# Normalised rows transposed by the DMA crossbar as fp16 halves, in place of TensorE in fp32

## The chip, the cores and the metric

The kernel runs on one core of a Trainium2 chip. A core has five engines that run programs of their own: TensorE (matrix products; PE in the profile, its weight loads PEld), VectorE (DVE), ScalarE (ACT), GpSimd (POOL) and SyncE (SP), which here does nothing but issue DMAs. They wait for each other on semaphores. The metric is the device time of one execution in microseconds (us); before the change it is 2462.75 us, the median of three runs (2460.89 to 2462.85).

## The reference

Input are 128 graphs of 128 nodes with 256 features (`x`) and their adjacency matrices. After a LayerNorm and a ReLU three layers follow, and the input is added at the end:

```
for l in range(3):
    scores = leaky(x@attn_w[l,:d] [:, :, None] + x@attn_w[l,d:] [:, None, :] + attn_b[l])
    attn = softmax(where(mask, scores, -inf))
    h = layernorm(x + attn @ x, g1[l], beta1[l])
    x = layernorm(h + gelu(h @ W1[l] + b1[l]) @ W2[l] + b2[l], g2[l], beta2[l])
```

Everything is float32. W1 is 256 x 1024 and W2 1024 x 256.

## The kernel before

Four graphs (T = 4) make a group; a group in one layer is an item, with 512 rows. There are 32 groups and 96 items. They are taken in rings of four groups: four items of layer 0, four of layer 1, four of layer 2, so twelve slots (PER) make one ring. Products are done in fp16 with both operands split into a high and a low half (hi = fp16(v), lo = v - hi), as three products hi*hi, hi*lo and lo*hi.

A software pipeline over slots sets the order. In slot s every engine goes through eight chunks c = 0..7. At each chunk TensorE does `hidden(s, c)`: 128 of the 1024 hidden features for the 512 rows, six matmuls (L369) with the transposed normalised rows `hT_hi`, `hT_lo` as moving operand; the first four use `hT_hi`, the last two `hT_lo`, and at c = 0 each pair is preceded by a wait for its half. ScalarE makes the GELU (L481) and the high half (L486), VectorE the low half (L573), and TensorE does `feed` of the chunk three earlier (12 matmuls, L383). Between the chunks stands the work of other items:

- item s+2: dot products for the scores on VectorE (L614, L617, c = 1), their spread over the rows by TensorE (L407, c = 4), scores, row maxima and `minus_max` on VectorE (L632 to L642, c = 4), leaky scores and exponentials on ScalarE (L509, L514, c = 5), the transpose of the probabilities on TensorE (L413, c = 7), their split (L519, L666), and in the next slot at c = 0, after `feed`, the aggregation (L425). VectorE then makes `res1` (L656) and its statistics (L580).
- item s+1: inverse deviation on GpSimd (L789, L791), `norm1` on ScalarE (L491, c = 2), its transpose on TensorE (`transpose_norm1`, L435, c = 4), `hT_hi` on ScalarE (L535, c = 4), `hT_lo` on VectorE (L671, c = 5), and on GpSimd the residual (L801, L803). The transpose is eight 128 x 128 transposes in fp32 into four PSUM banks of `p_pair`, which are shared with `feed` and the aggregation, so it waits for `res2` of item s-1.
- item s-1: residual `res2` (L681), statistics, normalisation and output on VectorE and GpSimd (L815, L827, L829, and L836 after the last layer).
- item s+4, where a new group starts (layer 0, `starts` in VectorE's program, four slots of twelve): statistics of the input and mask on VectorE (L580, L601, L604).

PSUM is full: three banks for `hidden`, one for the scores and probabilities, four for `p_pair`.

SyncE's program is written group by group: it waits until `x_in` and `adj_in` of a group are used up and loads the group two further on, then waits for an output, stores it, and loads `x` again for the sum at the end. Within the loop its addresses come from a register.

The lines of the prediction's steps are those named above; the waits of the low half at TensorE are L367 and L368, and the six matmuls of a chunk are issued in the loop at L365.

Of the kernel before, what the change touches and what calls it, by code (L numbers as in the profile page):

```python
# [35 lines left out]
P = 128  # L36
B, N, D = 128, 128, 256
L = 3
# [21 lines left out]
def layer_of(s):  # L60
    return (s % PER) // RING
# [35 lines left out]


def is_item(r, s):
    return not isinstance(r, int) or 0 <= PER * r + s < ITEMS  # L100
# [29 lines left out]
def gnn_kernel(nc, x, adj, attn_w, attn_b, W1, b1, W2, b2, g1, beta1, g2, beta2, out):  # L130
    with ExitStack() as ctx:
# [55 lines left out]
        h_res = [sb(f"h_res{i}", [P, T, D]) for i in range(2)]  # L187
        hT_hi = [sb(f"hT_hi{i}", [P, KD, TN], F16) for i in range(2)]
        hT_lo = [sb(f"hT_lo{i}", [P, KD, TN], F16) for i in range(2)]
        g_hi = [sb(f"g_hi{i}", [P, TN], F16) for i in range(GS_RING)]  # L190
# [20 lines left out]
        def ff_banks(s):  # L211
            return p_pair[s % 2]

        def nT_banks(s):
            return p_pair[s % 2][:].rearrange("p (k u) d -> p k (u d)", k=KD)

# [31 lines left out]
        norm1_ready = sem("norm1_ready")  # L248
        nT_psum = sem("nT_psum")
        hT_hi_ready = sem("hT_hi_ready")  # L250
# [23 lines left out]
        @block.sync  # L274
        def _(sp):
            def weights(l):
                if l >= 1:
                    sp.wait_ge(w_lo_ready, 4 * l - 2)
                    sp.wait_ge(bias_psum, l)
                sp.dma_start(w1_f32[:], W1[l].rearrange("(k p) h -> p k h", p=P)).then_inc(w_dma[0], 16)  # L280
                if l >= 1:
                    sp.wait_ge(w_lo_ready, 4 * l)
                sp.dma_start(w2_f32[:], W2[l].rearrange("(c p) d -> p c d", p=P)).then_inc(w_dma[1], 16)

            def graphs(tensor, g):

                v = tensor.rearrange("(g t) n d -> n g t d", t=T)
                if isinstance(g, int):
                    return v[:, g]
                return v[:, bass.ds(g, 1)].rearrange("n g t d -> n (g t) d")  # L290

            def load_x(g, i):
                sp.dma_start(x_in[i][:], graphs(x, g)).then_inc(x_loaded[i], 16)

            def load_adj(g, i):
                sp.dma_start(adj_in[i][:], graphs(adj, g)).then_inc(adj_loaded[i], 16)

            def load_again(g, i):
                sp.dma_start(x_again[i][:], graphs(x, g)).then_inc(x_again_loaded[i], 16)

            def store(g, i):
                sp.dma_start(graphs(out, g), y_out[i][:]).then_inc(stored[i], 16)

            load_x(0, 0)
            load_adj(0, 0)
# [7 lines left out]
            load_x(1, 1)  # L313
            load_adj(1, 1)
            weights(0)
            for g in (2, 3, 4, 5):
                sp.wait_ge(x0_ready, 4 * (g - 1))
                load_x(g, g % 2)
                sp.wait_ge(mask_steps, 2 * (g - 1))
                load_adj(g, g % 2)  # L320
                if g == 2:
                    for dst, v in ((g1_rows, g1), (b2_rows, b2), (res_rows, beta1), (g2_rows, g2), (beta2_rows, beta2)):
                        sp.dma_start(dst[:].rearrange("p l d -> p (l d)"),
                                     flat(v).partition_broadcast(P)).then_inc(rows_dma, 16)
                if g in (3, 4):
                    weights(g - RING + 2)
            load_again(0, 0)
            load_again(1, 1)

            for r in range(LOOPS - 1):  # L330
                for q in range(RING):
                    i, g = q % 2, r * RING + q

                    sp.wait_ge(x0_ready, r * (4 * RING) + 4 * (RING + q + 1))
                    load_x(g + (RING + 2), i)
                    sp.wait_ge(mask_steps, r * (2 * RING) + 2 * (RING + q + 1))
                    load_adj(g + (RING + 2), i)

                    sp.wait_ge(x_steps, x_total(r, 2 * RING + q, 5))
                    store(g, i)  # L340
                    load_again(g + 2, i)
            for g in range(RING * (LOOPS - 1), G):
                if g + RING + 2 < G:
                    sp.wait_ge(x0_ready, 4 * (g + RING + 1))
                    load_x(g + RING + 2, g % 2)
                    sp.wait_ge(mask_steps, 2 * (g + RING + 1))
                    load_adj(g + RING + 2, g % 2)
                sp.wait_ge(x_steps, x_total(g // RING, 2 * RING + g % RING, 5))
                store(g, g % 2)
                if g + 2 < G:  # L350
                    load_again(g + 2, g % 2)
            for i in range(2):
                sp.wait_ge(stored[i], 16 * G // 2)

        @block.tensor
        def _(pe):
            def hidden(r, s, c):

                l, i = layer_of(s), s % 2
                if c == 0:  # L360
                    pe.wait_ge(hT_hi_ready, total(r, s, 1, 1))
                if later(r, s) or c >= PF_RING:
                    pe.wait_ge(g_lo_ready, total(r, s, C, c + 1 - PF_RING))
                cols = slice(c * P, (c + 1) * P)
                for n, (w, h, k) in enumerate((w, h, k) for w, h in ((w1_hi, hT_hi), (w1_lo, hT_hi), (w1_hi, hT_lo))  # L365
                                              for k in range(KD)):
                    if c == 0 and n == 2 * KD:  # L367
                        pe.wait_ge(hT_lo_ready, total(r, s, 1, 1))  # L368
                    mm = pe.matmul(p_hid[in_ring(s, c, PF_RING)][:], w[l][:, k, cols], h[i][:, k, :],  # L369
                                   start=(n == 0), stop=(n == 3 * KD - 1))  # L370
# [45 lines left out]
            def aggregate(r, s):  # L416

                pe.wait_ge(pT_lo_ready, total(r, s, 1, 1))
                pe.wait_ge(X_lo_ready, total(r, s, 1, 1))
                if later(r, s):  # L420
                    pe.wait_ge(hT_lo_ready, total(r, s - 1, 1, 1))
                for t in range(T):
# [16 lines left out]
            def slot(r, s):  # L439
                for c in range(C):  # L440
# [13 lines left out]
                    if c == 4 and first:  # L454
                        spread_sj(r, s + 2)
                    if c == 4 and is_item(r, s + 1):
                        transpose_norm1(r, s + 1)
                    if c == 4 and is_item(r, s + 2) and not first:
# [8 lines left out]
        def _(act):  # L467
# [61 lines left out]

            def high_hT(r, s):  # L530

                act.wait_ge(nT_psum, total(r, s, 1, 1))
                if later(r, s, 2):
                    act.wait_ge(hid_psum, total(r, s - 2, C, C))
                act.activation(hT_hi[s % 2][:], nT_banks(s), ACT.Copy).then_inc(hT_hi_ready, 1)  # L535

            def slot(r, s):
                if isinstance(r, int) and r == 0 and s in (0, 3):
                    act.wait_ge(bias_ready, 1 if s == 0 else L)
                for c in range(C):  # L540
# [8 lines left out]
                    if c == 4 and is_item(r, s + 1):  # L549
                        high_hT(r, s + 1)  # L550
                    if c == 5 and is_item(r, s + 2):
# [9 lines left out]
        def _(dve):  # L561
# [106 lines left out]

            def split_hT(r, s):
                dve.wait_ge(hT_hi_ready, total(r, s, 1, 1))  # L670
                dve.tensor_tensor(hT_lo[s % 2][:], nT_banks(s), hT_hi[s % 2][:], ALU.subtract).then_inc(hT_lo_ready, 1)  # L671

# [33 lines left out]
            def slot(r, s):  # L706
# [7 lines left out]
                for c in range(C):  # L714
# [33 lines left out]
                    if c == 5 and is_item(r, s + 1):  # L748
                        split_hT(r, s + 1)
                    if c == 5 and starts and not late:  # L750
# [128 lines left out]
```

## Time and profile before

| | us |
|---|---|
| median of 3 runs | 2462.75 |
| the profiled execution | 2464.22 |
| its span | 2462.4 |
| TensorE busy | 2350.7 (95%) |
| VectorE busy | 2097.8 (85%) |
| ScalarE busy | 1890.0 (77%) |
| GpSimd busy | 1701.0 (69%) |

The granted TensorE clock is 0.993 of full speed over the span. An engine's busy time doesn't say whether it sets the time; that is read from the chain of waits, which follows the last instruction back through what released it. The rows are below.

### The profile page before, as it was taken

The page shows a single profiled execution, that of the slowest core. Times are in us where ns is not written, and L with a number is a line of the kernel's source. Part 1 is how long each engine was busy: PE and PEld are TensorE (multiplying, and loading weights), DVE is VectorE, ACT ScalarE, POOL GpSimd, SP SyncE. Part 2 cuts the span into 40 slices and gives each one's busy share as a digit, 9 for nine tenths or more (in the row PEclk, how much of TensorE's full clock was granted, in tenths as well). Part 3 has the DMA queues.
Part 4 walks back from the last instruction along what each step waited for, and adds up shares of the span by engine and source line. Part 5 has one row for each costly group of instructions (what it writes and reads, how often), then busy time and mean ns, then how long its engine had stood idle before and what let it go on. Part 6 is the DMA issues. An engine that isn't in the chain of part 4 may idle for free.

```text
span 2462.4 us, 47718 instructions
## 1 busy us (share of the span) xinstructions
PE 2350.7 (95%) x16608; PEld 1648.4 (67%) x16608; DVE 2097.8 (85%) x6070; ACT 1890.0 (77%) x3402; POOL 1701.0 (69%) x1540
## 2 busy tenths in 40 slices
PE   3999999999999999999999999999999999999997
PEld 2766666676666666667666666666666666666765
DVE  6778998888988899888988889988898889988884
ACT  4767788877787878787787777877778777878783
POOL 3457677767776767766786667776678676777675
PEclk9999999999999999999999999999999999999998
DMA  5200012000210002100021001200012000110001
GB/s 170 73 1 1 1 44 78 1 1 1 74 48 1 1 14 61 48 1 1 14 78 31 1 1 31 73 18 2 1 44 61 18 2 1 44 52 1 1 1 52
DMA packets 77422, 70.84 MB, mean 29 GB/s; under 512 B 7040, under 2 KB 75648, under 8 KB 77184
## 3 DMA queue, kind: packets, MB, share of 16 engines
q1 hardware_dynamic: 77184, 67.79, 9.1%
q8 instruction: 134, 2.20, 0.4%
q14 instruction: 104, 0.85, 0.1%
HBM read 51.01 MB, written 16.78 MB: 28 GB/s over the span
## 4 chain that ended last, share of the span: by engine, by line
DVE 55%; PE 19%; ACT 13%; issue 10%; POOL 0%; DVEq 0%; POOLq 0%
DVE g_lo L573 11%; DVE bn L580 9%; PE p_pair L383 8%; DVE res L656 6%; DVE dots L614 6%; ACT probs L514 5%; PE p_hid L369 5%; ACT L514 5%; DVE res L681 5%; DVE scores L632 4%; DVE dots L617 4%; PE p_pair L425 3%; DVE row_top L638 3%; DVE minus_max L642 2%; PE p_att L413 2%
## 5 line engine op out<-in xcount | busy, mean ns | idle before, releaser
L383 PE MATMUL p_pair<-w_hi,g_hi 128*128 128x256 f16 x3072 | 839.1, 273 | 0.0
L383 PE MATMUL p_pair<-w_lo,g_hi 128*128 128x256 f16 x3072 | 838.8, 273 | 0.0
L383 PE MATMUL p_pair<-w_hi,g_lo 128*128 128x256 f16 x3072 | 838.8, 273 | 0.0
L481 ACT ACTIVATE p_hid<-p_hid,b_eff 128x512 f32<-128x512 f32 x768 | 504.5, 657 | 328.6 <-PE p_hid L369 327.4
L573 DVE TENSOR_TENSOR g_lo<-p_hid,g_hi 128x512 f16<-128x512 f32 x768 | 527.5, 687 | 239.4 <-ACT g_hi L486 232.9
L801 POOL TENSOR_TENSOR h_res<-norm,g_rows 128x1024 f32<-128x1024 f32 x96 | 227.7, 2372 | 395.8 <-DVE res L681 389.1
L486 ACT ACTIVATE g_hi<-p_hid 128x512 f16<-128x512 f32 x768 | 458.5, 597 | 24.3
L369 PE MATMUL p_hid<-hT_hi,w_hi 128*128 128x512 f16 x1536 | 458.7, 380 | 2.3 <-DVE g_lo L573 2.3
L369 PE MATMUL p_hid<-hT_hi,w_lo 128*128 128x512 f16 x1536 | 458.9, 380 | 0.0
L369 PE MATMUL p_hid<-hT_lo,w_hi 128*128 128x512 f16 x1536 | 458.8, 380 | 0.0
L789 POOL TENSOR_TENSOR rstd<-var_eps,minus_half 128x4 f32<-128x4 f32 x224 | 241.6, 1079 | 307.4 <-DVE minus_mean L588 302.1
L383 PEld LDWEIGHTS p_pair<-w_lo,g_hi 128*128 128x128 f16 x3072 | 301.2, 98 | 107.3 <-issue 0.8
L383 PEld LDWEIGHTS p_pair<-w_hi,g_hi 128*128 128x128 f16 x3072 | 301.2, 98 | 106.2 <-issue 1.0
L383 PEld LDWEIGHTS p_pair<-w_hi,g_lo 128*128 128x128 f16 x3072 | 301.2, 98 | 35.5
L491 ACT ACTIVATE norm<-res,shift,rstd 128x256 f32<-128x256 f32 x384 | 199.3, 589 | 102.0 <-POOL shift L791 102.0
L369 PEld LDWEIGHTS p_hid<-hT_lo,w_hi 128*128 128x128 f16 x1536 | 150.8, 98 | 182.6 <-issue 2.5
L369 PEld LDWEIGHTS p_hid<-hT_hi,w_lo 128*128 128x128 f16 x1536 | 150.7, 98 | 182.5 <-issue 2.2
L580 DVE BATCH_NORM_STATS2 bn<-res 128x6 f32<-128x256 f32 x768 | 268.9, 414 | 3.3
L803 POOL TENSOR_TENSOR h_res<-h_res,res_rows 128x1024 f32<-128x1024 f32 x96 | 226.9, 2363 | 7.5
L587 DVE TENSOR_SCALAR var_eps<-mv 128x4 f32<-128x4 f32 x224 | 213.4, 953 | 7.7
L815 POOL TENSOR_SCALAR norm<-res,rstd,shift 128x256 f32<-128x256 f32 x384 | 209.8, 561 | 10.0
L656 DVE SCALAR_TENSOR_TENSOR res<-p_pair,row_inv,X 128x256 f32<-128x256 f32 x384 | 159.0, 477 | 65.5 <-PE p_pair L425 65.5
(67 smaller groups left out, 3855.2 us busy)
## 6 DMA issues: line engine op xcount, KB each, us to landing
x_in<-in_x SPq DMA_DIRECT2D x32, 512.0 KB, 5.3
x_again<-in_x SPq DMA_DIRECT2D x32, 512.0 KB, 5.1
out<-y_out SPq DMA_DIRECT2D x32, 512.0 KB, 3.3
adj_in<-in_adj SPq DMA_DIRECT2D x32, 256.0 KB, 5.6
w_f<-in_L_gnn_W SPq DMA_DIRECT2D x6, 1024.0 KB, 5.6
attn_rows<-in_L_gnn_attn_w SPq DMA_DIRECT2D x1, 768.0 KB, 5.6
g_rows<-in_L_gnn_g SPq DMA_DIRECT2D x2, 384.0 KB, 8.3
b_rows<-in_L_gnn_b SPq DMA_DIRECT2D x1, 384.0 KB, 7.4
```

Source lines behind the costliest of these rows:

```text
L369: mm = pe.matmul(p_hid[in_ring(s, c, PF_RING)][:], w[l][:, k, cols], h[i][:, k, :], start=(n == 0), stop=(n == 3 * KD - 1))
L383: mm = pe.matmul(ff_banks(s)[:, t, :], g[i][:, nodes], w[l][:, c, :], start=(c == 0 and t % 2 == 0 and n == 0), stop=(c == C - 1 and n == ...
L481: act.activation(p_hid[k][:], p_hid[k][:], ACT.Gelu, bias=b1_eff[:, l, c:c + 1], scale=1.0 / WSCALE).then_inc(gelu_ready, 1)
L486: act.activation(g_hi[i][:], p_hid[k][:], ACT.Copy).then_inc(g_hi_ready, 1)
L514: act.activation(probs[:, t, :], leaky[:, t, :], ACT.Exp, bias=minus_max[:, t:t + 1], accum_out=row_sum[:, t:t + 1]).then_inc(probs_ready, 1)
L573: dve.tensor_tensor(g_lo[i][:], p_hid[k][:], g_hi[i][:], ALU.subtract).then_inc(g_lo_ready, 1)
L580: dve.bn_stats(bn[n][:, t, :], src[:, t, :]).then_inc(stat_steps[n], 1)
L587: dve.tensor_scalar(var_eps[n][:], mv[n][:, :, 1], EPS, None, ALU.add).then_inc(stat_steps[n], 1)
L656: dve.scalar_tensor_tensor(out=res1[:, t, :], in0=agg_banks(s)[:, t, :], scalar=row_inv[:, t:t + 1], in1=X[s % RING][:, t, :], op0=ALU.mul ...
L789: pool.tensor_tensor(rstd[n][s % 2][:], var_eps[n][:], minus_half[:], ALU.pow).then_inc(rstd_ready[n], 1)
L801: pool.tensor_tensor(h_res[i][:], norm1[:], rows(g1_rows, l, T), ALU.mult).then_inc(h_res_steps, 1)
L803: pool.tensor_tensor(h_res[i][:], h_res[i][:], rows(res_rows, l, T), ALU.add).then_inc(h_res_steps, 1)
```

## The change

TensorE's `transpose_norm1` is gone. ScalarE makes `h_hi` = fp16(`norm1`) and VectorE `h_lo` = `norm1` - `h_hi` as they lie, nodes on partitions, in SBUF. SyncE then issues for each half a transposing DMA from SBUF to SBUF, which writes `hT_hi` or `hT_lo`, now laid out as [feature, graph, k, node]. TensorE waits for the DMAs' semaphores (16 each) at the same places as before. `h_hi` and `h_lo` have one buffer each, the `hT` two. The aggregation now waits for `res2` three items back, in place of `hT_lo` of the item before. SyncE's program is written in the same slots as the other engines', since its transposes come once a slot; the loads and stores stand ahead of them in the slot, except W2's and the first two loads of `x` again.

```diff
+            def turn_h(r, s):
+                i = s % 2
+                if later(r, s, 2):
+                    sp.wait_ge(hid_psum, total(r, s - 2, C, C))
+                for h, hT, made, turned in ((h_hi, hT_hi, h_hi_ready, hT_hi_ready), (h_lo, hT_lo, h_lo_ready, hT_lo_ready)):
+                    sp.wait_ge(made, total(r, s, 1, 1))
+                    sp.dma_start_transpose(hT[i][:].rearrange("p t k n -> p (t k) n"),
+                                           h[:].rearrange("p t d -> p (t d)")).then_inc(turned, 16)
+            def slot(r, s):
+                if is_item(r, s + 2) and layer_of(s + 2) == 0 and group_of(r, s + 2) + 2 < G:
+                    sp.wait_ge(x0_ready, group_total(r, s + 2, 4, 4))
+                    load_x(group_of(r, s + 2) + 2)
+                if is_item(r, s + 3) and layer_of(s + 3) == 0 and group_of(r, s + 3) + 2 < G:
+                    sp.wait_ge(mask_steps, group_total(r, s + 3, 2, 2))
+                    load_adj(group_of(r, s + 3) + 2)
...
+                if is_item(r, s - 3) and layer_of(s - 3) == L - 1:
+                    store(r, s - 3)
+                if is_item(r, s + 1):
+                    turn_h(r, s + 1)
...
+            slots(sp, slot)
...
                 if c == 0:
-                    pe.wait_ge(hT_hi_ready, total(r, s, 1, 1))
+                    pe.wait_ge(hT_hi_ready, total(r, s, 16, 16))
...
                     if c == 0 and n == 2 * KD:
-                        pe.wait_ge(hT_lo_ready, total(r, s, 1, 1))
-                    mm = pe.matmul(p_hid[in_ring(s, c, PF_RING)][:], w[l][:, k, cols], h[i][:, k, :],
+                        pe.wait_ge(hT_lo_ready, total(r, s, 16, 16))
+                    mm = pe.matmul(p_hid[in_ring(s, c, PF_RING)][:], w[l][:, k, cols], h[i][:, :, k, :],
...
-                if later(r, s):
-                    pe.wait_ge(hT_lo_ready, total(r, s - 1, 1, 1))
+                if later(r, s, 3):
+                    pe.wait_ge(res2_ready, total(r, s - 3, 2, 2))
...
-            def transpose_norm1(r, s):
-                if later(r, s, 2):
-                    pe.wait_ge(res2_ready, total(r, s - 2, 2, 2))
-                pe.wait_ge(norm1_ready, total(r, s, 4, 4))
-                for k in range(KD):
-                    for t in range(T):
-                        mm = pe.transpose(nT_banks(s)[:, k, t * N:(t + 1) * N],
-                                          norm1[:, t, k * P:(k + 1) * P], ident[:])
-                mm.then_inc(nT_psum, 1)
...
                 if later(r, s):
-                    act.wait_ge(nT_psum, total(r, s - 1, 1, 1))
+                    act.wait_ge(h_lo_ready, total(r, s - 1, 1, 1))
...
-                act.activation(hT_hi[s % 2][:], nT_banks(s), ACT.Copy).then_inc(hT_hi_ready, 1)
+            def high_h(r, s):
+                act.wait_ge(norm1_ready, total(r, s, 4, 4))
+                if later(r, s):
+                    act.wait_ge(hT_hi_ready, total(r, s - 1, 16, 16))
+                act.activation(h_hi[:], norm1[:], ACT.Copy).then_inc(h_hi_ready, 1)
...
-                dve.tensor_tensor(hT_lo[s % 2][:], nT_banks(s), hT_hi[s % 2][:], ALU.subtract).then_inc(hT_lo_ready, 1)
+            def low_h(r, s):
+                dve.wait_ge(h_hi_ready, total(r, s, 1, 1))
+                if later(r, s):
+                    dve.wait_ge(hT_lo_ready, total(r, s - 1, 16, 16))
+                dve.tensor_tensor(h_lo[:], norm1[:], h_hi[:], ALU.subtract).then_inc(h_lo_ready, 1)
```

## Rows read from the trace of the kernel before

**Rows 1.** The page: busy time, share of the span; chain that ended last.
```profile
PE 2350.7 (95%) x16608; PEld 1648.4 (67%) x16608; DVE 2097.8 (85%) x6070; ACT 1890.0 (77%) x3402; POOL 1701.0 (69%) x1540
...
DVE 55%; PE 19%; ACT 13%; issue 10%; POOL 0%; DVEq 0%; POOLq 0%
```
**Rows 2.** Stretches: length; busy PE, PEld, DVE, ACT, POOL; PEclk. Plain slot, new-group slot.
```profile
1098.47:1122.83 24.36, 24.11 (x174) 16.97 (x173) 20.47 (x60) 18.99 (x35) 16.42 (x15) 1.00 0.01 1
1197.16:1222.75 25.59, 24.33 (x174) 16.91 (x172) 24.15 (x72) 20.73 (x39) 18.03 (x17) 1.00 0.10 32
```
**Rows 3.** The chain of waits, 1113 to 1140: start, length, what.
```profile
1113.88 1.67 DVE res L656 x4
...
1128.09 0.58 DVE minus_max L642
...
1130.94 1.35 ACT probs L514 x7
...
1132.34 0.66 PE p_att L413 x4
...
1138.26 1.67 DVE res L656 x4
```
**Rows 4.** Waits of the run: total us, times, longest.
```profile
PE p_att L413 <- ACT probs L514: 44.4, 94, 4.5
...
PE p_pair L435 <- DVE res L681: 20.3, 28, 1.1
```
**Rows 5.** Timeline, 1186 to 1188, a slot with a new group: start, length.
```profile
1186.66 0.27 PE L425 MATMUL p_pair<-X_hi,pT_lo 128*128 128x256 f16 x1
...
1187.18 1.26 DVE L656 SCALAR_TENSOR_TENSOR res<-p_pair,row_inv,X 128x256 f32<-128x256 f32 x3
```
**Rows 6.** Timeline of TensorE at chunk 4 of a plain slot.
```profile
1099.73 1.04 PE L435 MATMUL p_pair<-ident,norm 128*128 128x128 f32 x8
```
**Rows 7.** Timeline of the same slot, from the halves to the next slot.
```profile
1100.81 1.02 ACT L535 ACTIVATE hT_hi<-p_pair 128x1024 f16<-128x1024 f32 x1
...
1106.96 1.21 DVE L671 TENSOR_TENSOR hT_lo<-p_pair,hT_hi 128x1024 f16<-128x1024 f32 x1
...
1109.66 0.21 PEld L369 LDWEIGHTS p_hid<-hT_hi,w_hi 128*128 128x128 f16 x2
...
1110.42 0.31 PEld L369 LDWEIGHTS p_hid<-hT_lo,w_hi 128*128 128x128 f16 x2
1110.55 0.69 DVE L573 TENSOR_TENSOR g_lo<-p_hid,g_hi 128x512 f16<-128x512 f32 x1 [2.38 <-ACT g_hi L486]
```
**Rows 8.** Timeline of the start-up: VectorE's weight splits beside GpSimd.
```profile
49.26 2.12 POOL L807 TENSOR_TENSOR X_lo<-X,X_hi 128x1024 f16<-128x1024 f32 x1
49.89 2.57 DVE L566 SCALAR_TENSOR_TENSOR w_lo<-w_f,w_hi 128x1024 f16<-128x1024 f32 x1
...
53.70 1.45 POOL L789 TENSOR_TENSOR rstd<-var_eps,minus_half 128x4 f32<-128x4 f32 x1 [2.32 <-DVE minus_mean L588]
54.65 1.22 DVE L566 SCALAR_TENSOR_TENSOR w_lo<-w_f,w_hi 128x1024 f16<-128x1024 f32 x1
```
**Rows 9.** DMA issues: KB, us to landing; last row from 1500 to 1520.
```profile
out<-y_out SPq DMA_DIRECT2D x32, 512.0 KB, 3.3
adj_in<-in_adj SPq DMA_DIRECT2D x32, 256.0 KB, 5.6
...
beta_rows<-in_L_gnn_beta SPq DMA_DIRECT2D x1, 384.0 KB, 8.8
...
adj_in<-in_adj SPq DMA_DIRECT2D x1, 256.0 KB, 4.3
```
**Rows 10.** TensorE by stretch (PEclk third from the end), and after a long wait.
```profile
60.00:90.00 30.00, 29.74 (x187) 0.83 0.22 71
...
165.00:171.00 6.00, 5.84 (x32) 0.72 0.00 0
...
165.16 0.66 PE L413 MATMUL p_att<-ident,probs 128*128 128x128 f32 x4 [4.25 <-ACT probs L514]
```

More of the change, by code:

```diff
@@ L96, in x_total, with group_of @@
     return (4 * PER + RING) * r + v if isinstance(r, int) else r * (4 * PER + RING) + v
+def group_of(r, s):
+    return RING * (r + s // PER) + s % RING
 def is_item(r, s):
@@ L187, in gnn_kernel @@
         h_res = [sb(f"h_res{i}", [P, T, D]) for i in range(2)]
-        hT_hi = [sb(f"hT_hi{i}", [P, KD, TN], F16) for i in range(2)]
-        hT_lo = [sb(f"hT_lo{i}", [P, KD, TN], F16) for i in range(2)]
+        h_hi, h_lo = sb("h_hi", [P, T, D], F16), sb("h_lo", [P, T, D], F16)
+        hT_hi = [sb(f"hT_hi{i}", [P, T, KD, N], F16) for i in range(2)]
+        hT_lo = [sb(f"hT_lo{i}", [P, T, KD, N], F16) for i in range(2)]
         g_hi = [sb(f"g_hi{i}", [P, TN], F16) for i in range(GS_RING)]
@@ L212, in ff_banks @@
             return p_pair[s % 2]
-        def nT_banks(s):
-            return p_pair[s % 2][:].rearrange("p (k u) d -> p k (u d)", k=KD)
         def agg_banks(s):
@@ L248, in gnn_kernel @@
         norm1_ready = sem("norm1_ready")
-        nT_psum = sem("nT_psum")
+        h_hi_ready = sem("h_hi_ready")
+        h_lo_ready = sem("h_lo_ready")
         hT_hi_ready = sem("hT_hi_ready")
@@ L275, in _, with weights @@
         def _(sp):
-            def weights(l):
+            def weights(l, n):
                 if l >= 1:
-                    sp.wait_ge(w_lo_ready, 4 * l - 2)
+                    sp.wait_ge(w_lo_ready, 4 * l - 2 + 2 * n)
+                if l >= 1 and n == 0:
                     sp.wait_ge(bias_psum, l)
[L280 to L283, printed above, removed]
+                if n == 0:
+                    sp.dma_start(w1_f32[:], W1[l].rearrange("(k p) h -> p k h", p=P)).then_inc(w_dma[0], 16)
+                else:
+                    sp.dma_start(w2_f32[:], W2[l].rearrange("(c p) d -> p c d", p=P)).then_inc(w_dma[1], 16)
@@ L285, in graphs @@
             def graphs(tensor, g):
[L287 to L305, printed above, removed]
+                return tensor.rearrange("(g t) n d -> n g t d", t=T)[:, g]
+            def load_x(g):
+                sp.dma_start(x_in[g % 2][:], graphs(x, g)).then_inc(x_loaded[g % 2], 16)
+            def load_adj(g):
+                sp.dma_start(adj_in[g % 2][:], graphs(adj, g)).then_inc(adj_loaded[g % 2], 16)
+            def load_again(g):
+                sp.dma_start(x_again[g % 2][:], graphs(x, g)).then_inc(x_again_loaded[g % 2], 16)
@@ new lines, in store @@
+            def store(r, s):
+                g = group_of(r, s)
+                sp.wait_ge(x_steps, x_total(r, s, 5))
+                sp.dma_start(graphs(out, g), y_out[g % 2][:]).then_inc(stored[g % 2], 16)
+                if g + 2 < G:
+                    load_again(g + 2)
+            def turn_h(r, s):
[6 more added lines that the diff above has]
+                                           h[:].rearrange("p t d -> p (t d)")).then_inc(turned, 16)
@@ new lines, in slot @@
+            def slot(r, s):
[5 more added lines that the diff above has]
+                    load_adj(group_of(r, s + 3) + 2)
+                if (r, s) == (0, -2):
+                    for dst, v in ((g1_rows, g1), (b2_rows, b2), (res_rows, beta1), (g2_rows, g2), (beta2_rows, beta2)):
+                        sp.dma_start(dst[:].rearrange("p l d -> p (l d)"),
+                                     flat(v).partition_broadcast(P)).then_inc(rows_dma, 16)
+                if (r, s) in ((0, -1), (0, 1)):
+                    weights((s + 3) // 2, 0)
+                if is_item(r, s - 3) and layer_of(s - 3) == L - 1:
+                    store(r, s - 3)
+                if is_item(r, s + 1):
+                    turn_h(r, s + 1)
+                if (r, s) in ((0, -1), (0, 1)):
+                    weights((s + 3) // 2, 1)
+                if (r, s) == (0, 2):
+                    load_again(0)
+                    load_again(1)
@@ L306, in _ @@
+            load_x(0)
+            load_adj(0)
             flat = lambda v: v.rearrange("l d -> (l d)")
@@ L312, in _ @@
                     sp.dma_start(dst[:], v.rearrange("l (c p) -> p l c", p=P)).then_inc(cols_dma, 16)
[L313 to L351, printed above, removed]
+            load_x(1)
+            load_adj(1)
+            weights(0, 0)
+            weights(0, 1)
+            slots(sp, slot)
+            for s in range(PER - 2, PER):
+                store(LOOPS, s)
             for i in range(2):
@@ L455, in slot @@
                         spread_sj(r, s + 2)
-                    if c == 4 and is_item(r, s + 1):
-                        transpose_norm1(r, s + 1)
                     if c == 4 and is_item(r, s + 2) and not first:
@@ L528, in high_X @@
                 act.activation(X_hi[:], X[s % RING][:], ACT.Copy).then_inc(X_hi_ready, 1)
[L530 to L534, printed above, removed]
-                act.activation(hT_hi[s % 2][:], nT_banks(s), ACT.Copy).then_inc(hT_hi_ready, 1)
+            def high_h(r, s):
[3 more added lines that the diff above has]
+                act.activation(h_hi[:], norm1[:], ACT.Copy).then_inc(h_hi_ready, 1)
             def slot(r, s):
@@ L549, in slot @@
                     if c == 4 and is_item(r, s + 1):
-                        high_hT(r, s + 1)
+                        high_h(r, s + 1)
                     if c == 5 and is_item(r, s + 2):
@@ L748, in slot @@
                     if c == 5 and is_item(r, s + 1):
-                        split_hT(r, s + 1)
+                        low_h(r, s + 1)
                     if c == 5 and starts and not late:
```

2 lines of the change are left out of this document (removed).

## The prediction

> **What bounds the kernel now.** I read the page's busy shares first, then its chain of waits, then single slots. The shares point at TensorE: it is busy for 95% of the span, VectorE for 85% [rows 1]. The chain says something else: 55% of it is VectorE, 19% TensorE, 13% ScalarE [rows 1]. Two slots of the middle show why. A plain slot takes 24.36 us, one in which a new group's input statistics and mask are made takes 25.59 us [rows 2]; there are four of the second kind in every twelve (`starts` in VectorE's program). In a plain slot one loop closes, and the chain gives its pieces [rows 3]: VectorE goes from `res1` (L656, 1113.88) without a pause to `minus_max` (L642, ends 1128.67), 14.8 us; ScalarE makes leaky scores, loads a table and makes four exponentials, until 1132.29, 3.6 us; TensorE transposes the probabilities at 1132.34 and then does feed chunk 4, hidden chunk 0 of the next slot, feed chunk 5 and the aggregation, 5.9 us, until VectorE's next `res1` at 1138.26. 14.8 + 3.6 + 5.9 = 24.4 us, the whole slot. The part of TensorE's work that the change removes, the eight fp32 transposes at L435, stands at chunk 4. That stretch of TensorE's program is not in the loop: TensorE arrives at the probabilities and waits for them, in 94 slots, 44.4 us in all [rows 4]. So TensorE is nearly full, but it has no say on the part that is lightened.
>
> In a slot of the second kind the loop is longer and leaves TensorE out (ScalarE goes on with the GELU of chunk 6 and VectorE waits for that), but only just: the last aggregation matmul ends at 1186.93 and `res1` starts at 1187.18, a slack of 0.25 us [rows 5].
>
> **Part 1: the eight transposes go, and the wait for `res2` before them.** On TensorE they take at most 1.04 us a slot [rows 6], 96 x 1.04 = 100 us, and their wait 20.3 us over the run [rows 4]. Next late in their place is the wait for the probabilities, which grows by the same amount. I count 0 for the steady slots. Only where TensorE itself is the pace does it help: in the start-up, with the clock at 0.83 between 60 and 90 us and no idle time worth naming [rows 10]; two such slots, about 1.5 us each: -3 us. Bounds for this part: -120 us (100 + 20.3, all of it on the path) and 0.
>
> **Part 2: the two halves are made from SBUF.** ScalarE's copy is the same size (`hT_hi`, 1.02 us [rows 7]) and needs only `norm1`, ready long before; nothing. VectorE's subtraction stays where it was, at chunk 5, after 3.9 us of other work behind `minus_max`; it took 1.21 us and ended at 1108.17 [rows 7]. Now both its inputs lie in SBUF. The weight splits (L566) have that form and width: 1.22 us when GpSimd ran the small L789 beside them, 2.57 us when GpSimd's wide L807 was in progress (it ended just when the extra 1.3 us were over) [rows 8]. At chunk 5 GpSimd is at L789, so I take 1.21, with 1.35 us more as the upper bound. It lies in VectorE's idle time ahead of g_lo of chunk 6 (2.38 us, [rows 7]; 1.1 us in the other slots). GpSimd may be held back by it: its L789 took 1.45 us there [rows 8]; some 0.5 us, inside idle time of its own (its mean idle share is 31%, [rows 1]).
>
> The new waits on single buffers cost nothing: `high_h` (behind it on ScalarE: the exponentials) waits for the high transpose of the item before, issued a slot earlier; `low_h` (behind it: g_lo of chunk 6) waits for a low half that TensorE needed at this slot's chunk 0; the aggregation's wait for `res2` is two slots old.
>
> **Part 3: the crossbar.** Per slot SyncE issues two transfers of 256 KB. The high half is ready at 1101.9 and first needed at 1109.66, when TensorE loads weights for hidden chunk 0 of the next slot: 7.8 us [rows 7]. The low half is ready at 1108.17 and needed at 1110.42, at the fifth of the six matmuls of that chunk: only 2.25 us, where before there were the same 2.25 us and no transfer in between. And this point is inside the loop: behind the waiting matmul stand feed chunk 5 and the aggregation, and VectorE's `res1` waits for them. Every microsecond that the landing takes beyond about 2.2 us comes on top of the slot.
>
> No row of the trace is a transpose or moves SBUF to SBUF. The nearest: `adj_in`, 256 KB, lands 5.6 us after its issue (median), and 4.3 us in a quiet stretch, behind one other load [rows 9]; the store, which reads SBUF, lands 512 KB in 3.3 us [rows 9]. Half the bytes would land after half of that, 1.65 us, if all of it were moving, and after 3.3 us if none were; the middle of the two, 2.5 us, is my lower end. The longest landing of the page is 8.8 us (a broadcast load, the last of five) [rows 9]: upper end. I take 5.0 us, halfway between the quiet and the median row of the same size: the SBUF source speaks for less, turning two-byte elements for more. The wait is 5.0 - 2.2 = 2.8 us.
>
> The Trainium skill ("DMA: Bandwidth & Descriptors", section on the anatomy of one DMA) gives a DMA a fixed cost of about 2.0 us plus bytes over 436 GB/s. By it, as an estimate, 256 KB would land in 2.6 us, close to my lower end, and the sum would be about 2490 us.
>
> **Part 4: SyncE's program in slots.** Loads and stores keep their conditions and stand ahead of the slot's two transposes. The low half of a slot is issued at chunk 5 to 6; the next `load_x` can go only after `norm_input` at chunk 7. The four of a slot are issued and landed (3.3 to 5.6 us each, [rows 9]) before chunk 4, where `h_hi` appears, ten microseconds into the slot. 0, and up to 1 us in a slot if a load is still moving when a transpose is issued. If the waits on `x_steps` came late, the transposes behind them on SyncE's queue would be late too; they are released in the slot before.
>
> **The sum**, against the profiled execution's 2464.2 us (1.5 us above the median of 2462.75, which is nothing here). Of the 95 handovers from slot to slot two lie in the slow-clocked start-up. 61 plain ones x 2.8 = 171 us, 32 of the other kind x (2.8 - 0.25) = 82 us, start-up -3 us: 2464 + 250 = about **2713 us**, 10% slower. With the low end of 2.5 us: 61 x 0.3 + 32 x 0.05 = 20, less 3: 2481 us. With 3.3: 2555. With 8.8: 61 x 6.6 + 32 x 6.35 = 606: 3067 us.
>
> **Rivals.**
> (a) The landing fits into the gap (2.2 us or less). Then TensorE's 1.04 us turn into waiting for the probabilities and only the start-up gains: about 2461 us, no change. For it: same loop, nothing else added. Against: no DMA row under 3.3 us. 6%.
> (b) TensorE is the bound after all, as its 95% suggest, and the lighter chunk 4 comes through: 2464 - 120 = 2344 us. It decides if the landing fits and the wait for the probabilities shrinks instead of growing. Against: the loop closes without L435 to 0.1 us. 4%.
> (c) The new idle time costs clock. After TensorE's idle time of 4.25 us up to 165.16 the granted clock was 0.72 over the next 6 us [rows 10], part of it at the lower of the two levels (1.2 in place of 2.4 GHz): 6 x 0.28 = 1.7 us lost. Idle time in a slot would be 1.3 us before the probabilities and 2.8 us at the low half. If each slot pays it: 93 x 1.7 = 158 us, 2871 us. 14%; at the 5.0 us landing the longest single gap is still shorter than that row's.
> (d) The crossbar is far slower than a plain transfer and lands after more than 8.8 us: from 3067 us, and with the clock of (c) 3225 us. Past 7.8 us the high half is late too. For it: the transfer is in two-byte elements, unlike any row. 11%. The Trainium skill ("VectorE: DVE Perf Modes", the three transpose paths) puts a 128x128 bf16 block at 1309 ns through the crossbar against 390 ns on TensorE, and advises TensorE where a PSUM destination will do. Taken block by block for the eight blocks, an estimate, that is 10.5 us and 61 x 8.3 + 32 x 8.05 = 764 us more, 3225 us; no row here shows it.
>
> **How the numbers follow.** The forecast (landing 2.5 to 8.8 us, clock kept) has 65%. Its own range is 2481 to 3067 us and holds (c) as well; what is left outside are (a), (b), (d) and a landing a little over 2.2 us, some 2 in 10. Differences under 0.2% (5 us) can't be told from no change. Faster: (b) and a part of (a) with a good start-up, 5%; same 5%; slower 90%.
>
> **What would show it.** In the profile after: waits of PE at L369 for the DMA into `hT_lo` in nearly every slot, 2 to 4 us each, and none for `hT_hi`; PE's wait for the probabilities up from 44 to some 130 us; no L435; VectorE's `low_h` at 1.2 us; the chain of waits with DMA in it; plain slots near 27 us; the landing of the 256 KB transposes near 5 us. Wrong if slots are 24.4 us or shorter, if the wait is for `hT_hi` or for a load queued ahead, or if the landing is outside 2.5 to 8.8 us.

## The result and the profile after

The changed kernel takes 2514.86 us, median of 4 runs (2514.32 to 2516.94); the kernel before took 2461.82 us in the same batch (2460.57 to 2462.85). The ratio is 1.0217, with a 95% interval of 1.02 to 1.0235: 2.2% slower. The direction and the mechanism were forecast, the size was not: 53 us lost instead of 250.

The page of the kernel after, its busy shares and its chain that ended last:
```profile
PE 2282.2 (91%) x15840; PEld 1561.1 (62%) x15840; DVE 2093.1 (83%) x6070; ACT 1886.7 (75%) x3402; POOL 1744.5 (69%) x1540
...
DVE 58%; PE 16%; issue 11%; DMA 8%; ACT 6%; SPq 0%; POOL 0%; POOLq 0%; DVEq 0%
```
Against [rows 1], TensorE is 68.5 us less busy and the span is 50 us longer (2512.4 after 2462.4). DMA has come into the chain with 8%. VectorE is as busy as before, GpSimd 43.5 us more.

Its waits (total us, times, longest), to set beside [rows 4]:
```profile
PE p_att L417 <- ACT probs L506: 132.8, 94, 4.9
...
PEld p_hid L373 <- DMA hT_lo<-h_lo: 91.9, 86, 2.2
...
PE p_hid L373 <- DMA hT_lo<-h_lo: 37.9, 63, 1.7
```
The wait for the probabilities went from 44.4 to 132.8 us, which is where most of TensorE's spared work went (88 us of at most 100). The new wait is for the low half, in 86 of the 95 handovers. For `hT_hi` there is a single one of 0.4 us, in the start-up.

Its DMA issues (KB where the record has them, us to landing):
```profile
hT_hi<-h_hi SPq DMA_TRANSPOSE x96, 3.0
hT_lo<-h_lo SPq DMA_TRANSPOSE x96, 3.1
```
The landing I had taken as 5.0 us is 3.1 us.

Three stretches of the kernel after, with the columns of [rows 2]: a plain slot, a new-group slot without output, a new-group slot in which an output is finished (the skip connection, GpSimd's L829):
```profile
1093.81:1118.89 25.08, 23.42 (x166) 16.01 (x165) 20.48 (x60) 18.93 (x35) 16.84 (x15) 1.00 0.17 23
1219.78:1245.39 25.61, 23.43 (x167) 16.03 (x165) 23.78 (x72) 20.76 (x40) 18.48 (x17) 1.00 0.20 52
1245.39:1271.46 26.07, 23.85 (x171) 16.39 (x169) 24.63 (x72) 20.76 (x39) 20.80 (x18) 1.00 0.36 92
```
Before, the three took 24.36, 25.60 and 25.65 us. So a plain slot loses 0.73 us, a new-group slot nothing or 0.43 us. Slot by slot over the two traces (a slot runs from one `X_hi` copy to the next): 61 plain slots +47.3 us, 14 new-group slots without output +0.2, 14 with output +6.0, start-up -3.4 (the first copy 2.4 us later, the six slots behind it 5.85 us shorter). The sum is +50.1; the spans differ by 50.0. A few of the plain slots lose more than 0.73: in one of 26.11 us the low half was late by another microsecond, in two of 26.0 us the granted clock was 0.93.

**The plain slot.** The chain of the kernel after, from the last piece before the exponentials to the next `res1` (start, length, what):
```profile
1099.06 0.56 DVE minus_max L633
...
1101.79 0.59 DVE g_lo L564
1102.38 1.14 DVE h_lo L664
...
1103.54 3.09 DMA hT_lo<-h_lo
...
1106.68 0.60 PE p_hid L373 x2
1107.28 1.31 PE p_pair L387 x12
1108.59 1.32 PE p_pair L429 x12
...
1109.94 1.67 DVE res L647 x4
```
In [rows 3] the way from `minus_max` to `res1` went over ScalarE's exponentials and TensorE's transposes of the probabilities. Now it goes over VectorE's `low_h` and the transfer, because that branch ends later. By how much is read from the timeline of the same slot:
```profile
1102.30 1.21 DVE L664 TENSOR_TENSOR h_lo<-norm,h_hi 128x1024 f16<-128x1024 f32 x1
...
1103.30 0.66 PE L417 MATMUL p_att<-ident,probs 128*128 128x128 f32 x4 [1.12 <-ACT probs L506]
1103.54 1.23 SPq L315 DMA_TRANSPOSE hT_lo<-h_lo  x1
...
1106.68 0.60 PE L373 MATMUL p_hid<-hT_lo,w_hi 128*128 128x512 f16 x2 [0.55 <-DMA hT_lo<-h_lo]
```
In the kernel before, the slot of [rows 7]:
```profile
1107.96 0.66 PE L413 MATMUL p_att<-ident,probs 128*128 128x128 f32 x4 [0.25 <-ACT probs L514]
...
1110.63 0.59 PE L369 MATMUL p_hid<-hT_lo,w_hi 128*128 128x512 f16 x2
```
There the first low product ran 2.67 us after the transposes of the probabilities began. Here that would be 1103.30 + 2.67 = 1105.97; it runs at 1106.68, 0.71 us late, and the slot is 0.73 us longer. The gap that the transfer had to fit into was 1105.97 - 1103.54 = 2.43 us. The row of the wait says 0.55, less than 0.71: a wait's row alone undercounts what the slot loses, since the modelled end of the matmul before reaches into it (two such matmuls are shown as 0.59 us long, and the next two start after 0.43). TensorE arrives at the probabilities early and waits 1.12 us, but that is the other branch.

**The new-group slot with output.** GpSimd in the kernel after, in the third stretch:
```profile
1253.45 1.02 POOL L782 TENSOR_TENSOR rstd<-var_eps,minus_half 128x4 f32<-128x4 f32 x1 [0.17 <-DVE minus_mean L579]
1254.54 0.61 POOL L784 TENSOR_TENSOR shift<-minus_mean,rstd 128x4 f32<-128x4 f32 x1
1255.26 2.18 POOL L808 TENSOR_SCALAR norm<-res,rstd,shift 128x256 f32<-128x256 f32 x4
1257.40 2.35 POOL L829 TENSOR_TENSOR y_out<-y_out,x_again 128x1024 f32<-128x1024 f32 x1
```
and VectorE behind it:
```profile
1259.14 0.63 DVE L578 TENSOR_SCALAR var_eps<-mv 128x4 f32<-128x4 f32 x1
1259.68 0.16 DVE L579 TENSOR_SCALAR minus_mean<-mv 128x4 f32<-128x4 f32 x1
```
`low_h` (1253.88 to 1255.09) runs beside the `shift`. In the same slot of the kernel before, VectorE and GpSimd:
```profile
1231.24 1.21 DVE L671 TENSOR_TENSOR hT_lo<-p_pair,hT_hi 128x1024 f16<-128x1024 f32 x1
...
1236.51 0.20 DVE L587 TENSOR_SCALAR var_eps<-mv 128x4 f32<-128x4 f32 x1
```
```profile
1231.90 0.20 POOL L791 TENSOR_TENSOR shift<-minus_mean,rstd 128x4 f32<-128x4 f32 x1
...
1234.34 2.34 POOL L836 TENSOR_TENSOR y_out<-y_out,x_again 128x1024 f32<-128x1024 f32 x1
```
The subtraction took the same 1.21 us with one input in PSUM, and the `shift` beside it took 0.20 us. With both inputs in SBUF the `shift`, which starts while it runs, takes 0.61 and ends just behind it; the `rstd`, which was under way when it started, keeps its 1.02. Everything behind it on GpSimd is 0.4 us later. `var_eps` on VectorE, which took 0.20 us before, now comes while L829 is running, takes 0.63 and ends as L829 ends (1259.77 and 1259.75), and the slot, whose pace VectorE sets, is 0.43 us longer.

### The profile page after: what moved, and what is told of

Its sections match the earlier page's. It is cut to its first block, busy times and chain, and to the rows that moved or that the text cites. A ratio compares the mean times of both kernels' runs of the same rounds, so it can differ in the third digit from the quotient of the medians.

```text
span 2512.4 us, 46470 instructions
## 1 busy us (share of the span) xinstructions
PE 2282.2 (91%) x15840; PEld 1561.1 (62%) x15840; DVE 2093.1 (83%) x6070; ACT 1886.7 (75%) x3402; POOL 1744.5 (69%) x1540
## 2 busy tenths in 40 slices
DMA packets 280171, 121.12 MB, mean 48 GB/s; under 512 B 209792, under 2 KB 278400, under 8 KB 279936
## 3 DMA queue, kind: packets, MB, share of 16 engines
q1 hardware_dynamic: 279936, 118.15, 19.9%
## 4 chain that ended last, share of the span: by engine, by line
DVE 58%; PE 16%; issue 11%; DMA 8%; ACT 6%; SPq 0%; POOL 0%; POOLq 0%; DVEq 0%
DVE g_lo L564 12%; DVE bn L571 9%; DMA hT_lo<-h_lo 8%; PE p_pair L387 7%; DVE res L647 6%; DVE dots L605 6%; PE p_pair L429 5%; DVE res L674 4%; DVE scores L623 4%; DVE dots L608 4%; PE p_hid L373 4%; DVE h_lo L664 3%; DVE row_top L629 3%; DVE minus_max L633 2%; DVE mv L576 2%
## 5 line engine op out<-in xcount | busy, mean ns | idle before, releaser
L373 PEld LDWEIGHTS p_hid<-hT_lo,w_hi 128*128 128x128 f16 x1536 | 143.9, 98 | 254.5 <-DMA hT_lo<-h_lo 91.9
L578 DVE TENSOR_SCALAR var_eps<-mv 128x4 f32<-128x4 f32 x224 | 207.4, 926 | 7.7
```

Of the source, the lines that this page charges most:

```text
L578: dve.tensor_scalar(var_eps[n][:], mv[n][:, :, 1], EPS, None, ALU.add).then_inc(stat_steps[n], 1)
```

## The experiments

Seven kernels are the changed or the earlier kernel with one edit, one (low_after_stats) has two. There were two batches: beside experiments 1 to 4 the kernel before had a median of 2462.15 us, beside 5 to 8 one of 2463.47. Ratios are against the kernel before of the same batch. Slots are compared in the profiled executions.

**1. TensorE's transposes back in (e1_te_back).** Their result is not used; the crossbar's halves are.
```diff
+def transpose_norm1(r, s):            # the 8 fp32 transposes of before
+    ...
     if c == 4 and is_item(r, s + 1):
+        transpose_norm1(r, s + 1)
     ...                               # ScalarE, norm_attention
+    act.wait_ge(nT_psum, total(r, s - 1, 1, 1))
```


> The changed kernel with TensorE's eight fp32 transposes of norm1 put back at chunk 4, beside the DMA's; their result is not used. Theory (the loop closes over the probabilities, the transposes lie outside it): the changed kernel's time of 2515 us stays within 8 us, the start-up giving back a few; TensorE's wait for the probabilities falls from 133 us to about 50. Rival (the change has two large parts, a loss of some 150 us by the late low half and a gain of some 100 us on TensorE): about 2600 us, the gain undone.

2513.7 us, ratio 1.0205 (1.019 to 1.022), 1 us from the changed kernel. Its waits:
```profile
PEld p_hid L377 <- DMA hT_lo<-h_lo: 96.5, 92, 2.1
...
PE p_att L421 <- ACT probs L523: 43.4, 94, 4.5
PE p_hid L377 <- DMA hT_lo<-h_lo: 40.0, 69, 1.7
```
The wait for the probabilities falls from 132.8 back to 43.4 us, the waits for the low half stay, and a plain slot still loses 0.70 us. 100 us of TensorE's work at chunk 4 are worth nothing in the steady slots, in or out.

**2. The low half is transferred twice (e5_low_twice).** The spare copy stands ahead of the real one.
```diff
     sp.wait_ge(made, total(r, s, 1, 1))
+    if h is h_lo:
+        sp.dma_start_transpose(hT_spare[:].rearrange("p t k n -> p (t k) n"),
+                               h[:].rearrange("p t d -> p (t d)")).then_inc(turned, 16)
     sp.dma_start_transpose(...
     ...                               # TensorE and VectorE: 32 in place of 16
```


> The changed kernel with a second transpose of the low half into a spare tile queued ahead of the real one; TensorE waits for both. This doubles the suspected cost. Theory: issue of the first takes SyncE 1.23 us, so the last lands 1.3 to 1.9 us later (4.4 to 5.0 us after the first issue); each plain slot grows by as much, new-group slots by 0.3 to 1: 2515 + 61 x 1.6 + 32 x 0.6 = about 2630 us. This is also the landing of 5.0 us on which the forecast of 2713 us was built, so it tells whether the forecast's other terms were right. Rival (slots absorb a late landing): under 2560 us.

2669.69 us, ratio 1.084 (1.081 to 1.087): slower than expected. Two plain slots of this kernel (columns as above, PEclk third from the end):
```profile
1428.32:1454.76 26.44, 23.41 (x166) 15.97 (x165) 20.48 (x60) 19.03 (x36) 16.81 (x15) 1.00 0.16 31
1562.31:1590.47 28.16, 25.08 (x166) 16.74 (x165) 20.46 (x60) 19.03 (x35) 16.79 (x15) 0.94 0.15 29
```
The first kind, 38 of 61, is 2.1 us over the kernel before: 0.7, and 1.4 because the low half now lands 4.5 us after the first issue in place of 3.1. The second kind, 23 of 61, is 3.8 over it. It does the same 166 matmuls, 1.67 us slower, at a granted clock of 0.94, which is a mean: part of the slot ran at the lower of the two levels (1.2 in place of 2.4 GHz). This is rival (c) of the prediction: its price was 1.7 us a slot, and at these waits a third of the slots pay it. The two kinds don't differ in their own waits (1.1 us for the probabilities, 2.0 for the low half in most slots of both), so which slot pays is not told by the slot itself.

This is also a test of the prediction's sum. For a landing of 4.5 us it gives 2464 + 61 x 2.3 + 32 x 2.05 - 3 = 2667 us, close to the 2669.69, but partly by luck: the plain slots lose 169 us where the sum has 140 (39 of the 169 are clock), the new-group slots 39 where it has 66.

**3. The low half is made first (e2_low_first).** At chunk 5 VectorE does `low_h` ahead of the hidden part's g_lo.
```diff
+    if c == 5 and is_item(r, s + 1):
+        low_h(r, s + 1)
     if is_item(r, s):
         hidden(r, s, c)
     ...
-    if c == 5 and is_item(r, s + 1):
-        low_h(r, s + 1)
```


> The changed kernel with VectorE's low_h one instruction earlier, ahead of g_lo of chunk 5. Theory: the low half is issued 0.6 us sooner, a plain slot falls from 25.09 to about 24.5 us, and in the new-group slots with an output GpSimd's L784 is no longer held (0.2 in place of 0.6 us), so they fall from 26.07 to about 25.65: 61 x 0.6 + 14 x 0.4 = 42 us less, about 2473 us. Rival (the extra 0.43 us of these slots comes from stores and loads beside the transposes, not from L784): 26.07 stays, about 2479 us. Rival (the plain slots' 0.73 us is not the landing, but SBUF traffic or the clock): 2510 us or more.

2487.4 us, ratio 1.0106 (1.0088 to 1.0124). A plain slot is at +0.12 us against before, as expected. The new-group slot with output is not back at 25.65; it is at +0.91. GpSimd in that slot of this kernel:
```profile
1238.75 1.92 POOL L782 TENSOR_TENSOR rstd<-var_eps,minus_half 128x4 f32<-128x4 f32 x1 [0.18 <-DVE minus_mean L579]
1240.75 0.20 POOL L784 TENSOR_TENSOR shift<-minus_mean,rstd 128x4 f32<-128x4 f32 x1
```
Moved earlier, `low_h` (1238.59 to 1239.80) holds the `rstd` in place of the `shift`: 1.92 us instead of 1.02, 0.90 us, and the slot loses 0.91. Ten more us are in single slots behind the new-group ones; the costliest, of 27.21 us, had a granted clock of 0.87.

**4. The low products later (e3_low_later).** Chunk 0's two low products go behind feed chunk 5, 1.3 us later.
```diff
-    hidden(r, s, c)
+    hidden(r, s, c, (0,) if c == 0 else (0, 1))
     ...                               # feed chunk 5
+    if c == 0 and is_item(r, s):
+        hidden(r, s, c, (1,))         # the two products with hT_lo
     if c == 0 and is_item(r, s + 1):
         aggregate(r, s + 1)
```


> The changed kernel, but at chunk 0 TensorE does the four products with the high half, then feed chunk 5, then the two products with the low half, then the aggregation: the same work in another order, the low half needed 1.3 us later. Theory: the wait for the low half is gone and plain slots return to 24.36 us as in the kernel before; the 0.43 us in the new-group slots with an output stay: 2515 - 61 x 0.73 = about 2470 us. Rival (traffic or clock, not the wait): 2505 us or more, plain slots near 25.1.

2479.32 us, ratio 1.0067 (1.0051 to 1.0084). Of 61 plain slots 47 are within 0.05 us of the kernel before, so the 0.73 us was the wait for the transfer and nothing else. The new-group slot with output keeps its +0.42, as it must if GpSimd's hold-up is its cause. The rest of the plain slots' sum, 11 us, is in the other 14. In twelve of them (8 us) the low half landed late, 3.9 to 4.8 us after its issue; in two (3 us) the granted clock was 0.93. One late low half is issued at 1687.69; the DMA queues of this kernel from 1684 to 1690 us (packets, MB, share):
```profile
q1 hardware_dynamic: 502, 0.13, 33.6%
q8 instruction: 1, 0.02, 1.3%
q14 instruction: 1, 0.01, 0.5%
```
Beside the transposes' 502 packets two load instructions. Counted over the seven traces with transposes: of 911 transposes with no instruction load, no other load and no store moving in the 3.1 us from their issue none landed after more than 3.3 us; of 417 with an instruction load beside them 162 took more than 3.5. So late landings go with instruction loads. No run takes these away, so that they are the cause is argued and not shown.

**5. The aggregation first (e6_agg_early).** As 4, but the aggregation goes ahead of the low products too: high products of chunk 0, feed chunk 5, aggregation, low products.
```diff
     if c == 0 and is_item(r, s + 1):
         aggregate(r, s + 1)
+    if c == 0 and is_item(r, s):
+        hidden(r, s, c, (1,))
```


> As e3_low_later, but the aggregation also goes ahead of the two products with the low half: high products of chunk 0, feed chunk 5, aggregation, low products. Theory (the slot is the loop over minus_max, probabilities and TensorE's tail up to the aggregation): the tail is 0.43 us shorter, a plain slot takes 24.36 - 0.43 = 23.93 us, new-group slots keep 25.60 and 26.05, since their loop leaves TensorE out: 2479 - 61 x 0.43 = about 2453 us. Here TensorE's freed 1.04 us a slot are worth something for the first time. Rival (TensorE's clock takes it back, as in single slots of e3): 2465 us or more.

2447.13 us, ratio 0.9929 (0.9916 to 0.9943): faster than the kernel before. A plain slot and a new-group slot with output of this kernel, and one of its slower slots:
```profile
1089.27:1113.20 23.93, 23.25 (x166) 16.06 (x165) 20.47 (x60) 19.03 (x35) 16.84 (x15) 1.00 0.12 23
1238.29:1264.35 26.06, 24.91 (x181) 17.50 (x180) 24.62 (x72) 20.75 (x39) 20.79 (x18) 1.00 0.33 91
...
671.00:697.87 26.87, 24.08 (x149) 15.79 (x148) 20.46 (x60) 20.89 (x40) 19.12 (x16) 0.87 0.36 79
```
24.36 - 0.43 = 23.93: the two low products, which took 0.43 us between the probabilities and the aggregation, are out of the loop. The slower slots, such as the third row, stand right behind the new-group ones; in four of them the granted clock was 0.87 or 0.93.

**6. The same order, without the change (e8_before_agg).** The kernel before, with the edit of 5 alone.


> The kernel before, with TensorE's order of e6_agg_early and nothing else: TensorE's transposes stay. Theory: the loop would allow 23.93 us for a plain slot, but TensorE had only 0.24 us of waiting in 24.36, so it becomes the bound at about 24.12: 2462 - 61 x 0.24 = about 2447 us, with no DMA, no tail of late landings and no held GpSimd against it. So the whole of the change would be worth less than nothing even then (e6 2453). Rival (TensorE wasn't near its bound): 2436 us or less.

2433.79 us, ratio 0.9882 (0.9868 to 0.9895). It is the best of all, 1.2% below the kernel before and 3.3% below the changed one (0.9882 / 1.0217 = 0.967). Its slots:
```profile
1106.84:1130.77 23.93, 23.93 (x174) 16.91 (x173) 20.47 (x60) 19.11 (x35) 16.45 (x15) 1.00 0.00 1
1205.90:1231.56 25.66, 24.43 (x175) 16.82 (x172) 24.21 (x72) 20.74 (x40) 20.38 (x18) 1.00 0.24 73
```
The expectation that TensorE would be the bound at 24.12 us was wrong: the same 174 matmuls that counted 24.11 us busy in [rows 2] fit into 23.93, since the records of matmuls overlap with modelled ends. TensorE shows no idle time there now, and the chain of this kernel has 59% PE. Counted from start to start, TensorE's wait in the slot of [rows 7] was 0.41 us and not the row's 0.25 (the two matmuls before it start at 1107.12 and give way after 0.43, the next starts at 1107.96), and 24.36 - 0.41 = 23.95: it had that much room and no more. Whether TensorE or the loop ends last at 23.93 us can't be told from it: the kernel of experiment 5, with 0.68 us of TensorE idle, has the same length, so the loop alone gives it. Its new-group slots are unchanged (within 0.02 us), which is 6 us over 14 slots that the kernel of experiment 5 pays for GpSimd; the rest of the 13 us between the two is single slots such as the one above at 0.87.

**7. Low half behind the input statistics (e7_low_after_stats).** The kernel of experiment 5, and in new-group slots `low_h` after `input_statistics`, so that GpSimd's small instructions are over when it comes.
```diff
-    if c == 5 and is_item(r, s + 1):
+    if c == 5 and is_item(r, s + 1) and not (starts and not late):
         low_h(r, s + 1)
     ...                               # input_statistics(r, s + 4)
+        if is_item(r, s + 1):
+            low_h(r, s + 1)
```


> As e6_agg_early, with VectorE's low_h in the new-group slots behind the input statistics, 1.4 us later, where it no longer runs beside GpSimd's L784. Theory (GpSimd's two small operations wait while low_h reads two SBUF tensors, and where the skip connection fills GpSimd the delay comes back to VectorE at var_eps): the 0.43 us of the 14 new-group slots with outputs go, 26.05 to about 25.65: 6 us under e6. Rival (low_h now holds back GpSimd's next operation instead): the same as e6, within 2 us; if the low half is then late at TensorE, slower than e6.

2456.3 us, ratio 0.9974 (0.9964 to 0.9984), worse than that of experiment 5. The slot with output is at +0.98 instead of back at 25.65:
```profile
1216.62:1243.25 26.63, 25.95 (x185) 17.78 (x184) 25.26 (x72) 20.79 (x40) 21.34 (x18) 1.00 0.39 90
```
Now it meets the normalisation of 128x256 tiles; GpSimd in that slot of this kernel:
```profile
1226.07 3.13 POOL L815 TENSOR_SCALAR norm<-res,rstd,shift 128x256 f32<-128x256 f32 x4
```
Its four pieces take 3.13 us instead of 2.17. Three places for `low_h` held GpSimd by 0.41, 0.90 and 0.96 us, and the slots lost 0.43, 0.91 and 0.98. In each of them `var_eps` ends within 0.03 us of L829, as above. The cause is settled by that proportion; the place for it that costs nothing was not found.

**8. SyncE's program in slots, alone (e4_sync_slots).** The kernel before with the loads and stores issued from the slot program, no transposes by DMA.
```diff
-def load_x(g, i):
-    sp.dma_start(x_in[i][:], graphs(x, g)).then_inc(x_loaded[i], 16)
+def load_x(g):
+    sp.dma_start(x_in[g % 2][:], graphs(x, g)).then_inc(x_loaded[g % 2], 16)
 ...
+def slot(r, s):
+    ...                                # load_x, load_adj and store, each under its condition
```


> The kernel before with SyncE's program in slots and nothing else: no transposes by DMA, TensorE's stay. Theory: loads and stores are issued in good time either way, 2462 us within 4 us. Rival (some of the 53 us is in SyncE's new order of loads and stores): 2470 us or more.

2462.25 us, ratio 0.9994 (0.9985 to 1.0003): nothing, as expected. Its landings did move:
```profile
out<-y_out SPq DMA_DIRECT2D x32, 512.0 KB, 5.3
adj_in<-in_adj SPq DMA_DIRECT2D x32, 256.0 KB, 4.4
```
Before they were 3.3 and 5.6 us [rows 9], in the changed kernel 4.9 and 4.2. So this shift comes with SyncE's new program and not with the transposes.

Not tried: the low half in two transposes, the first of which could land while the second is made.

## Why the prediction was right in kind and wrong in size

**What bounds the kernel: right.** The loop over VectorE, ScalarE's exponentials and TensorE's late half closes a plain slot. Experiments 5 and 6 took 0.43 us out of TensorE's piece of it and got 0.43 us a slot.

**Part 1 (transposes go: 0): right.** The wait for the probabilities was forecast at some 130 us and is 132.8; experiment 1 puts the work back for nothing. The start-up gained 3.4 us (forecast 3), and with the transposes back (experiment 1) it gained 0.1.

**Part 2 (`low_h`: 1.21 us, hidden; GpSimd held inside idle time of its own): half right.** 1.21 us it is. (The "3.9 us of other work" behind `minus_max` was misread: it is 2.7 us of other work, and 3.9 us to the end of the subtraction. Nothing hangs on it.) GpSimd is held by 0.41 us (I wrote some 0.5), but "inside idle time of its own" rested on its mean idle share of the whole run [rows 1]. In a slot with output GpSimd runs from `rstd` to L829 without a pause and VectorE's `var_eps` waits for the end of it. A cost of 14 x 0.43 = 6 us that I set at 0.

**Part 3 (landing 5.0 us, wait 2.8 us): the term that was mis-sized.** The landing is 3.1 us and the gap 2.43 us, so the wait is 0.7. 61 x 0.73 = 45 us where the sum had 171. I took the middle between two rows of loads that start in HBM (4.3 and 5.6 us, [rows 9]) although the only row that starts in SBUF was the store's: 3.3 us for twice the bytes. Had I taken that row as the nearest, the sum as I gave it was 2555. The prediction also gave the gap as 2.25 us, to the load of the weights; the matmul behind it is 0.2 us later, and a wait costs only from there. With the 3.1 us as measured the sum would have been 2464 + 61 x 0.9 + 32 x 0.65 - 3 = 2537; what is left to the 2514 is 8 us of the gap and 15 us of the slack that follows.

For the new-group slots the sum had 32 x 2.55 = 82 us. I had read one slack, the 0.25 us before `res1` [rows 5]. There is more: in a slot without output, `var_eps` behind it waited for GpSimd as well. VectorE before, in the slot of [rows 5]:
```profile
1191.32 1.20 DVE L587 TENSOR_SCALAR var_eps<-mv 128x4 f32<-128x4 f32 x1
```
An instruction of 0.2 us that takes 1.20: 1.0 us in which it is held. After, `res1` waits 0.42 us for the aggregation, and `var_eps` takes 0.70:
```profile
1214.44 0.70 DVE L578 TENSOR_SCALAR var_eps<-mv 128x4 f32<-128x4 f32 x1
```
The slot stays at 25.6 us. The slack is thus 0.25 + 1.0 us, and experiment 2 bears it out: where plain slots lose 2.1 us, 16 of the 28 new-group slots lose 0.8 to 0.95.

The Trainium skill ("DMA: Bandwidth & Descriptors", the section on the anatomy of one DMA) would have given 2.6 us and with it 2490 us: nearer than my own, and still 0.5 us short of the 3.1 that the rows show. That section describes DMAs issued by GpSimd, which the prediction didn't say; these are issued by SyncE. The Trainium skill ("VectorE: DVE Perf Modes", the three transpose paths) puts a 128x128 bf16 block at 1309 ns through the crossbar; here eight blocks land in 3.1 us, so they don't go one after the other at that price (8 x 1.309 = 10.5 us), and the 3225 us worked out from it was far off.

**Part 4 (SyncE in slots: 0): right**, by experiment 8.

**The rivals.** (a) and (b) fell: the landing is over the gap, and TensorE's spared time turned into waiting. (c) didn't decide in this kernel, whose clock is 0.991, but its price is right (experiment 2). (d) fell with the landing of 3.1 us. Of the signs I named, four held (no L435, the wait for the probabilities, `low_h` at 1.2 us, DMA in the chain). The wait stands where I put it, in front of the low products and not of the high ones, but at 0.7 us and not at 2 to 4; so plain slots are at 25.1 and not near 27 us.

## What to carry to other kernels

When a transfer is put into a loop, compare its landing with the gap at the place of first use, and take the landing from the row with the same source and the nearest kind, not from the middle of rows of another source. Even that row is no constant: the store's went from 3.3 to 5.3 us when only SyncE's program was rearranged (experiment 8). If the gap is short by less than a microsecond, change the order of the consumer before anything else: here two matmuls moved behind the aggregation were worth 1.2% in the kernel before and 2.8% in the changed one, which the change had made 2.2% slower. Idle time read as a mean over the run hides nothing in the slot where the engine has none.

## What the runs showed of the hardware

- A transpose by DMA of 128x1024 two-byte elements within SBUF held SyncE's queue for 1.23 us and landed after 3.0 to 3.1 us in the median; in the changed kernel 19 of 192 took more than 3.5 us, up to 4.7. 192 of them raised the packets of the run from 77422 to 280171, nearly all of the new ones under 512 B, and the busy share of that queue from 9.1% to 19.9%.
- Late landings went with instruction loads on the DMA queues: 162 of the 417 transposes that had one beside them, 0 of the 911 that had neither such a load nor one of the kernel's own loads and stores beside them (seven traces).
- A VectorE subtraction of 128x1024 with both inputs in SBUF (1.21 us) held the GpSimd instruction that started while it ran: 128x4 instructions by 0.41 and 0.90 us, one of four 128x256 ones by 0.96, each ending behind the subtraction. One that was already under way kept its length (`rstd`, 1.02 us, in all 90 cases of the changed kernel). With one input in PSUM, as before, the 128x4 one beside it took its 0.20 us. The other way round, a VectorE instruction of 128x4 elements took up to 1.77 us while a wide one of GpSimd was under way.
- TensorE kept its full granted clock in 38 plain slots of experiment 2 and fell to a mean of 0.94 in 23, each time for 1.7 us of work, with waits of 1.1 us for the probabilities and 2 us for the low half in each slot. In the changed kernel, with 1.1 and 0.6 us, it fell in a few slots only.
